# A two-layer graph convolution with a routed feed-forward: sums with nodes on the lanes, and the second weight matrix applied in layer one

## The reference, cut to what matters

```python
x = x + gnn(layernorm(x), W1, b1, W2, b2, edge_weight, src, dst)      # x is 12500 x 256
x = x + routed_ffn(layernorm(x))                                      # 8 experts, hidden width 1024

def gcn_layer(x, W, b, edge_weight, src, dst):                        # 200000 edges, sorted by dst
    support = x @ W                                                   # W is 256 x 256
    msgs = support[src] * edge_weight[:, None]
    return segment_sum(msgs, dst, 12500) + b
h = elu(gcn_layer(x, W1, b1, ...))
h = elu(gcn_layer(h, W2, b2, ...))
```

## Time and profile before

| | us |
|---|---|
| median of three runs (lowest, highest) | 5709.33 (5689.48, 5714.56) |
| the profiled execution | 5730.26 |
| its span | 5728.4 |
| busy in it: PE, POOL, DVE, ACT | 3652.3, 3269.0, 2030.1, 1139.8 |
| first gather of layer one, of layer two, last product of layer two (about) | 87, 2444, 5150 |

### The profile page before, as it was taken

One profiled execution on the slowest core, in us unless ns is written; L12 is line 12 of the kernel. 1 busy time (PEld: TensorE's weight loads), 2 busy tenths in 40 slices (PEclk: granted clock), 3 DMA queues, 4 the chain that ended last, 5 costly groups with the idle time before them and its releaser, 6 DMA issues.

```text
span 5728.4 us, 84531 instructions
## 1 busy us (share of the span) xinstructions
PE 3652.3 (64%) x21450; PEld 3342.0 (58%) x21451; DVE 2030.1 (35%) x6619; ACT 1139.8 (20%) x1692; POOL 3269.0 (57%) x3403
## 2 busy tenths in 40 slices
PE   3455555555545555557667667667677666676999
PEld 2454455544545555446656666666666666665888
DVE  7222322322323322223333333333333333446333
ACT  3111111111101111013222222222222222230111
POOL 5666666666666666555555555655655555633444
PEclk6666666666666666667777777777777777778999
DMA  7333333333333333223333333333333333323554
GB/s 245 93 94 96 94 97 94 96 94 97 95 95 95 96 95 96 78 81 97 105 101 102 112 109 104 114 110 106 112 106 103 107 108 109 113 88 131 180 178 155
DMA packets 248229, 627.28 MB, mean 110 GB/s; under 512 B 63397, under 2 KB 110458, under 8 KB 247490
## 3 DMA queue, kind: packets, MB, share of 16 engines
q0 software_dynamic: 170688, 492.87, 29.8%
q1 hardware_dynamic: 76930, 129.30, 6.3%
HBM read 519.25 MB, written 103.63 MB: 109 GB/s over the span
## 4 chain that ended last, share of the span: by engine, by line
PE 40%; issue 22%; DVEq 3%; DVE 3%; ACT 1%; another core or an unknown queue 1%; DMA 0%; POOL 0%; ACTq 0%; POOLq 0%; SPq 0%
PE pB L1228 13%; PE pA L1187 13%; PE pA L1314 6%; PE pC L1210 3%; PE pZ L1197 2%; DVE S L862 1%; DVEq L862 1%; PE pC L1304 1%; PE pB L1304 1%; PE pZ L1221 1%; DVEq L890 0%; PE pT L1238 0%; PE pT L1216 0%; DVEq L903 0%
## 5 line engine op out<-in xcount | busy, mean ns | idle before, releaser
L1187 PE MATMUL pA<-S,rows 128*128 128x96 f32 x12544 | 1877.1, 314 | 1124.4 <-issue 786.0
L1187 PEld LDWEIGHTS pA<-S,rows 128*128 128x128 f32 x12544 | 1815.7, 230 | 1211.2 <-issue 881.6
L541 POOL DMA_INDIRECT rows<-h_scratch,idx x1568 | 1499.7, 956 | 1194.1 <-PE pA L1187 506.6
L541 POOL DMA_INDIRECT rows<-xn_scratch,idx x1568 | 1493.9, 953 | 832.2 <-issue 438.4
L1228 PE MATMUL pB<-work,w 128*128 128x128 f32 x3232 | 780.6, 374 | 738.6 <-issue 731.1
L1228 PEld LDWEIGHTS pB<-work,w 128*128 128x128 f32 x3232 | 644.9, 272 | 865.2 <-issue 863.9
L862 DVE TENSOR_SCALAR S<-iota_p,tdst,twgt 128x96 f32<-128x96 f32 x3168 | 888.4, 344 | 311.2 <-issue 294.8
L903 DVE TENSOR_TENSOR aggT<-aggT,pA 128x192 f32 x784 | 275.1, 351 | 1762.1 <-remote 907.7
L634 ACT ACT_TABLE_LOAD x196 | 251.5, 1283 | 1874.2 <-DVE aggT L903 883.8
L912 DVE TENSOR_TENSOR zb<-pZ,brow 128x256 f32<-128x256 f32 x198 | 84.0, 424 | 951.7 <-issue 556.9
L666 ACT ACTIVATE work<-pC 128x768 f32<-128x768 f32 x103 | 83.5, 811 | 1615.9 <-remote 1558.9
(11 more groups left out here) (177 smaller groups left out, 2158.3 us busy)
## 6 DMA issues: line engine op xcount, KB each, us to landing
pay_scratch<-work SPq DMA_DIRECT2D x98, 512.0 KB
rows<-xn_scratch,idx POOLq DMA_INDIRECT x1568
rows<-h_scratch,idx POOLq DMA_INDIRECT x1568
h_scratch<-work SPq DMA_DIRECT2D x98, 128.0 KB
pay_scratch<-work SPq DMA_DIRECT2D x98, 128.0 KB
work<-in_x_dram SPq DMA_DIRECT2D x97, 128.0 KB
rows<-in_x_dram SPq DMA_DIRECT2D x24, 512.0 KB, 5.7
xn_scratch<-rows SPq DMA_DIRECT2D x24, 512.0 KB, 6.3
```

What stands on the lines that cost most here:

```text
L541: pool.indirect_dma_start(rows[:, s, t, :], None, source, bass.IndirectOffsetOnAxis(at, 0))\
L1187: last = mm(to[:, k * W:(k + 1) * W], rows[:, slot, t, k * P:(k + 1) * P], Sx[:, t, :], start=(t == 0), stop=(t == T - 1))
```

## The change

1. **Products turned round.** S, now 128 columns wide, is the stationary operand and `rows[:, slot, t, :]` with all 256 features the moving one: 4 matmuls of 256 columns per group. The sums have nodes on the lanes and features along the row.
2. **Windows are blocks.** The sums live in `agg[node in block, block, 256]`. Lane n of S stands for the node n of the group's first block, or, if it is before the group's first node, for the node n of the next block. A group that spans at most 128 nodes is added twice with a column mask (0 or 1 per lane): once to its first block, once to the next (or to a dummy block). So DVE does two `scalar_tensor_tensor` of 256 columns per group in place of one add of 192.
3. **Scalars staged.** The table columns of a half are copied once to fixed places (`stage_cols`), so that the 16 S instructions of a half have no register offsets; S is built per pair of groups. One load brings all registers of a half (`half_regs`).
4. **W2 in layer one.** The tick of layer one transposes the block of sums (the product now needs it turned), multiplies with W1, forms h1, transposes h1, multiplies with W2 and stores h1 @ W2. Four ticks are in flight (`DEPTH1`), and four are run after the last half. In layer two the sums are already z: the tick has no `z_part`, and DVE reads `agg` directly.
5. The feed-forward's weights share the space of W1 and W2 and are loaded between the layers; the setup computes block numbers, masks and the table of registers.

```diff
-    W = 96
+    W = P
...
             def products(slot, Sx, to, semaphore):
 
-                for k in range(KC):
-                    for t in range(T):
-                        last = mm(to[:, k * W:(k + 1) * W], rows[:, slot, t, k * P:(k + 1) * P], Sx[:, t, :],
-                                  start=(t == 0), stop=(t == T - 1))
+                for t in range(T):
+                    last = mm(to, Sx[:, t, :], rows[:, slot, t, :], start=(t == 0), stop=(t == T - 1))
...
-                        to = aggT[:, :, bass.ds(bases[n], W)]
-                        v.tensor_tensor(to, to, group_sum(u + n).rearrange("p (k n) -> p k n", k=KC), ALU.add)\
-                         .then_inc(s_add[layer], 1)
-                        build_S(layer, g + n + HALF, u + n)
+                        for side in range(2):
+                            to = agg[:, bass.ds(bases[side * HALF + u + n], 1), :].rearrange("p b c -> p (b c)")
+                            last = v.scalar_tensor_tensor(out=to, in0=group_sum(u + n),
+                                                          scalar=cols[:, half, u + n, T + side:T + side + 1],
+                                                          in1=to, op0=ALU.mult, op1=ALU.add)
+                        last.then_inc(s_add[layer], 1)
+                    build_S(layer, g + HALF, 1 - half, u)
...
             def tick1(j):
-                z_part(0, j)
+                if flows(3, j):
+                    pe.wait_ge(s_stage2, j + 1)
+                    pe.wait_ge(s_s2, j + 1)
+                    for k in range(KC):
+                        last = mm(pZ2, stage2[:, k, :], wg2[:, k, :], start=(k == 0), stop=(k == KC - 1))
+                    last.then_inc(s_z2, 1)
...
+                if flows(0, j):
+                    pe.wait_ge(s_blk, j + 1)
+                    for k in range(KC):
+                        last = nc.tensor.transpose(pAT[:, k * P:(k + 1) * P], sums[:, k * P:(k + 1) * P], ident[:, :])
+                    last.then_inc(s_aT, 1)
+                if flows(2, j):
+                    pe.wait_ge(s_elu[0], j + 2)
+                    pe.wait_ge(s_stage2, j + 1)
+                    for k in range(KC):
+                        last = nc.tensor.transpose(pHT[:, k * P:(k + 1) * P], hout[:, k * P:(k + 1) * P], ident[:, :])
+                    last.then_inc(s_hT1, 1)
...
-                if flows(0, j):
-                    z_part(1, j)
```

More of the change, by code:

```diff
@@ L142, in bass_gnn_then_routed_ffn @@
         nmr = sb("nmr", [P, LNB, T])
[L143 to L144 removed]
+        zeros = sb("zeros", [P, 1])
         zneg = sb("zneg", [P, C])
@@ L154, in bass_gnn_then_routed_ffn @@
         hout = payh[:, 0:C]
+        stage, stage2 = (work[:, C * n:C * (n + 1)].rearrange("p (k n) -> p k n", k=KC) for n in range(2))
+        s2out, sums = work[:, 2 * C:3 * C], work[:, 3 * C:4 * C]
         bstat = sb("bstat", [P, 6])
@@ L355, in block_of, with sums_of, half_regs @@
             return bass.ds(j * -P + (NB - 1) * P, P)
+        def sums_of(j):
+            return agg[:, bass.ds(j * -1 + (NB - 1), 1), :].rearrange("p b c -> p (b c)")
         def flows(k, j):
             return not isinstance(j, int) or j - k < NB
+        def half_regs(eng, h, first, last):
+            _, values = nc.values_load_multi_w_load_instructions(
+                regs[0:1, bass.ds(h, 1), first:last].rearrange("a h r -> a (h r)"), engines=[eng.engine],
+                min_val=0, max_val=NB, skip_runtime_bounds_check_because=
+                "flags and numbers of blocks are at most the number of blocks")
+            return values
         def half_flags(eng, h):
-            v = eng.value_load(regs[0:1, bass.ds(h, 1), 0], min_val=0, max_val=(1 << 17) - 1)
-            return v >> 16, (v >> 8) & 255, v & 255
+            return half_regs(eng, h, 0, 3)
         def overflow_windows(eng, g):
@@ L680, in _ @@
                         h = 2 * i + half
[L681 to L684, removed]
+                        start, end = half_regs(act, h, 1, 3)
+                        ticks(act, start, end, (lambda j: tick1(j, h), tick2)[layer])
+                start, end = half_regs(act, NH, 1, 3)
+                ticks(act, start, end, (lambda j: tick1(j, NH), tick2)[layer])
                 if layer == 0:
-                    tick1(NB, None)
+                    for j in range(NB, NB + DEPTH1):
+                        tick1(j, NH)
             for j in range(NB, NB + DEPTH):
-                tick2(j, None)
+                tick2(j)
             act.wait_ge(s_dlog, 1)
@@ L984, in _ @@
                         stage_idx(layer, at, at)
-                    tc.then(v.memset(pC[:, :], 0.0))
                 dve.sem_inc(s_add[layer], HALF)
-                for u in range(HALF):
-                    build_S(layer, u, u)
+                for half in range(2):
+                    stage_cols(layer, half, half)
+                dve.wait_ge(s_cols[layer], 1)
+                dve.wait_ge(s_mm[layer], SLOTS)
+                for u in range(0, HALF, 2):
+                    build_S(layer, u, 0, u)
                 with dve.Fori(0, ITERS) as i:
@@ L1210, in tick2 @@
                     mm(pF[:, m // PERB, m % PERB, :], HT[:, m, :], identg[:, m, :], start=True, stop=True)
+                for m in range(FUSED, KH):
+                    last = mm(pLG, HT[:, m, :], identg[:, m, P:PG], start=(m == FUSED), stop=(m == KH - 1))
+                last.then_inc(s_log, 1)
                 if flows(3, j):
@@ L1269, in _ @@
                 ticks(pe, start, end, (tick1, tick2)[layer])
+                if layer == 0:
+                    for j in range(NB, NB + DEPTH1):
+                        tick1(j)
             for j in range(NB, NB + DEPTH):
```

317 lines of the change are left out of this document (175 added, 142 removed).

## The result

The changed kernel takes 6040.57 us (median of 4 runs, 6039.26 to 6045.42) beside 5699.4 us (5684.54 to 5714.56): a ratio of 1.060, 95% interval 1.0566 to 1.0634. The forecast was 5617 us, faster; the time lies above the whole range.

What follows compares the result with a forecast made beforehand. It took POOL's gather rhythm to bound layer one mostly, and PE's chain layer two. Terms +15 - 85 - 40 + 10 + 8 = -92 us gave 5617 us against the 5709.3 median; 8-in-10 range 5420 to 5770.

Steps and rivals of the forecast that it cites:

- So layer two pays for PE's work outside the starved stretch: Layer two: PE alone carries the chain outside times when all engines issue slowly during gathers; terms +15 and -85 us.
- The products: Layer two: 8 passes of 256 columns per group replace 16 of 96, 0.16 us more per half, +15 us.
- PE is at full clock at that place in the chain: Layer two's tick: reason for pricing the second-weights product at 0.87 us per half, not the half-clock 1.97.
- z in layer two: Layer two's tick: dropping the product with W2 saves 0.87 us per half, -85 us; bounds 0 and -193.
- Layer one: Layer one: PE's 3.0 us more per half is covered, under half of POOL's waits for PE go, -40 us.
- DVE: DVE's additions and S, both layers: 2.6 us more per half, covered by PE's idle time and slack, so 0.
- the sign of being wrong about DVE: Profile after: if PE's waits for DVE's additions grow, the forecast of 0 for DVE is wrong.
- Setup and seam: Before layer one, +10 us for extra DVE steps and masks; between layers, +8 us for four ticks running out.
- The starved stretches shrink: Rival, both layers: fewer PE and DVE instructions shrink slow-issue times and POOL's remote gaps; 5391 to 5524 us, chance 0.25.
- POOL's rhythm is the floor: Rival, both layers: POOL's gathers and gap set the time, PE's savings become waits; 5727 us, chance 0.16.
- PE becomes the bound of layer one: Rival, layer one's tick: 1.5 of PE's 3.0 us more per half show, +147 us; 5804 us, chance 0.13.
- the time of a pass is its columns: Rival, products of both layers: a third more columns takes a third more time; 6011 us, chance 0.04.

Runs made afterwards that it cites:

- e1: Changed kernel with a POOL pause of some 3 us before the fourth group's gathers in each half of layer two: 5545 us beside 5757 for the kernel before.
- e10: Changed kernel with 16 idle products (32 short passes) ahead of the fourth group in each half of layer two: 5637 us beside 5716 for the kernel before.
- e12: Changed kernel with a POOL pause after 8 gathers in each half of layer two: 5475 us beside 5716 for the kernel before.
- e3: Kernel before with only the turned product (8 passes of 256 columns per group, both layers); additions, S and ticks unchanged: 5968 us beside 5757.
- e4: Kernel before with the product by the second weights left out of layer two's tick and put nowhere: 5634 us beside 5757.
- e13: Changed kernel in which POOL's fourth group in layer two waits for a PE signal at the tick's end: 4692.5 us against 4661.1 for the kernel before.
- e5: Changed kernel with 16 idle products ahead of the fourth group in each half of layer two: 4699 us beside 4671 for the kernel before.
- e2: Changed kernel with 16 idle products (32 short passes) behind the products of each half of layer two: 6162 us beside 5757 for the kernel before.
- e18: Kernel before with a POOL pause after 12 gathers in each half of layer two: 5581 us beside 5746, a ratio of 0.972.

## Why the prediction was wrong

**The step that failed** is "So layer two pays for PE's work outside the starved stretch". It took the place and length of the stretch, and POOL's rhythm with it, as given, and let PE's savings count one for one: -70 us for layer two (+15 and -85), where the traces show +316. The sum lacks a term for what fewer instructions do to the rhythm. The rows for it were there: the stretches "end soon after POOL's run has ended", and remote gaps made 86.1 us per 1000. I counted those gaps as a loss that could only shrink. They were what ended the starvation: with runs of 16 it lasts longer, and PE's rest stands behind it with POOL silent. e1 and e10 gave the stop after 12 back and the loss went.

**The products**, +15 us: the price of a pass was right and the term wrong. In e12, 32 passes took 7.07 us at a granted clock of 1.00 (forecast 7.3):

```profile
3676.51 7.07 PE L1248 MATMUL pA<-rows,S 128*128 128x256 f32 x32
```

What they brought with them was some +186 us, by e3, through the fourth group's signal. The clock adds to it: "PE is at full clock at that place in the chain" no longer holds, as the window above with 0.50 shows. How much of the 316 us is the clock alone was not tried, nor how much the idle time in front of the products, for which the sum had no term.

**z in layer two**, -85 us: e4 measured 96 less in the layer. In the changed kernel z's place would be on the chain too, in the 3.6 us between the stretch and the products, but there PE's load of registers has come out from behind it. What is left of the 85 us was not measured.

**Layer one**, -40 us: measured -21. POOL's waits for PE fell from 40.8 to 29.8 us per 1000, the remote ones from 126.9 to 113.2:

```profile
POOL rows L566 <- remote: 113.2, 27, 5.1
...
POOL rows L566 <- PE pA L1243: 29.8, 12, 5.1
```

The runs grew here too, to 24 gathers in 33 cases, with fewer and longer gaps: 84 of 4.2 us in place of 126 of 3.05, 351 us in place of 384.

**DVE**, 0: four additions took 1.89 us (0.47 each, forecast 0.45), eight S about 2.12 (0.27, forecast 0.30). In layer two that was covered. In layer one the wait did not go but moved: from 1000 to 2000 us PE waited 138.2 us for the additions and 13.8 for S before, and now, with the additions ahead of S, this:

```profile
PE pA L1243 <- DVE S L912: 179.9, 47, 10.0
```

So the sign of being wrong about DVE is half there; that layer one got no slower means that POOL's rhythm covered it. **Setup and seam**, +18: measured +10, and 7 behind the layers that the sum had not.

**The rivals.** "The starved stretches shrink" was right that they would start later and that the remote gaps would go with fewer instructions, and had the sign wrong: the stretches grew with POOL's runs. "POOL's rhythm is the floor" is what happens on chips without starved stretches. "PE becomes the bound of layer one" and "the time of a pass is its columns" did not occur; 0.221 against 0.111 us a pass is a factor of 2.0 and not 2.67, as the rows before had it. None of the four was a stop of POOL whose loss costs time. The forecast's own range, 5530 to 5690, was also narrower than the bounds that it names: z alone spans 5617 - 108 = 5509 to 5617 + 85 = 5702. The measured time lies outside either.

## What to carry to other kernels

Where two engines hold each other up through a shared resource, a stop that looks like loss may be what lets the other work: before removing what causes it, ask how long the next undisturbed run will be, and what stands idle behind it. Where a releaser is called remote, compare the start of every engine that resumes at that moment; several at once, long after their producers, point to late signals and not to work. Prove such a theory by moving idle work rather than by removing work, and run the kernel before on the same chip each time. When work is taken off an engine, look also at what had been hidden behind it, down to its loads of registers.

## What the chip showed that was not expected

**Starved stretches came on some chips and not on others.** The kernel before took 5757, 5716, 5699 and 5746 us in four sets of runs, on three chips, and 4671 and 4661 us in two sets, on two other chips. Only one chip was met twice, with stretches both times, so a state that a chip has for a while is not ruled out. Without stretches POOL runs without a stop: 1568 gathers of layer two in 1986 us in e13, 1.27 us each, at a granted clock of 0.90 (2500 to 4000 us). Groups of e13, its gathers of layer two:

```profile
L569 POOL DMA_INDIRECT rows<-h_scratch,idx x1568 | 1509.8, 963 | 507.3 <-issue 494.2 <-PE pA L1247 12.8 <-PE pZ L1340 0.3
```

There e13 takes 4692.5 us against 4661.1, a ratio of 1.0065 (1.0048 to 1.0081). The changed kernel itself was not run on such a chip; e5 and e13, which contain it with a little more work, came out 0.6% and 0.7% above the kernel before, so its own loss there is likely no larger. The 6% belong to chips where the stretches occur, and no version here beats the kernel before on both kinds.

**A run of gathers stops PE after a number of instructions rather than after a time.** Take the long runs of layer two (12 gathers or more), and count from the first gather to PE's first idle gap of over 0.9 us that nothing in the profile explains. PE issued 119 passes and loads (standard deviation 8) in the kernel before, 110 (9) in the changed one, 108 (5) in e2, 117 (7) in e10 and 114 (15) in e18, while the mean time to it was 8.1, 9.5, 6.5, 7.3 and 7.8 us: the counts differ by 10%, the times by 46%. In layer one the counts scatter more: 93 (26) before and 89 (30) after the change. Whether the instructions of the other engines count too was not parted. Within a stretch, one instruction comes about each 0.7 us or a multiple of it (the load at 4022.84 and the pass at 4023.52 above). What is exhausted there, and why it differs between chips, stays open; so does whether recording the execution has a part in it, since each run on record was recorded with its granted clock.
